# Preparing the first unit of the state space layers between the groups of the gated expert stage before it, and down products one group later in both gated stages

## The reference

```python
x = x + 0.5 * _L1_ffn_ref(_layernorm(x), ...)     # m1a, gated experts
x = x + _L1_attn_ref(_layernorm(x), ...)          # mam, four state space layers
x = x + 0.5 * _L1_ffn_ref(_layernorm(x), ...)     # m1b, gated experts
```

```python
hidden = silu(gate_all) * up_all
out = einsum('nk,nkd->nd', combine, einsum('nke,ked->nkd', hidden, down_proj)) + shared(flat)
```

```python
x_in, z = split(layernorm(x) @ in_w.T)
xc = silu(conv4(x_in) + cb)
dtr, Bm, Cm = split(xc @ xp_w.T)
dt = softplus(dtr @ dt_w.T + dt_b)
h = h * exp(dt * A) + (dt * xc) * Bm     # a scan over the 256 rows, 16 states, 256 channels
y = sum(h * Cm) + xc * D
x = (y * silu(z)) @ out_w.T + x
```

## Time and profile before

| | us |
|---|---|
| median of 3 executions | 2748.93 (2746.9 to 2752.26) |
| profiled execution | 2750.35 |
| its span | 2748.6 |
| TensorE busy | 2499.3 (91%) |
| VectorE busy | 1939.4 (71%) |
| ScalarE busy | 1620.2 (59%) |
| GpSimd busy | 1144.2 (42%) |
| first gated stage, from the first gate product to the last add | 379.97 to 506.03 |
| last add to the second scan | 506.03 to 556.72 |
| state space stage to the second gated one | to 1403.48 |
| second gated stage, from its logits to the last transposes | 1403.48 to 1533.11 |

### The profile page before, as it was taken

The page is one execution under the profiler, slowest core; times in us unless marked ns, Lnnn a source line. Parts: engine busy times, 40 slices in busy tenths (PEclk is TensorE's granted clock), DMA queues, the critical chain, the costliest instruction groups (busy, mean ns, idle before and its releaser), DMA issues. The chain is left out here.

```text
span 2748.6 us, 37972 instructions
## 1 busy us (share of the span) xinstructions
PE 2499.3 (91%) x11190; PEld 1421.5 (52%) x11190; DVE 1939.4 (71%) x3923; ACT 1620.2 (59%) x3505; POOL 1144.2 (42%) x919
## 2 busy tenths in 40 slices
PE   7999978689999999999988899978879998799977
PEld 5766743345555555555434344446644445556655
DVE  6888856399999999999955444356644444587754
ACT  3565522388888888888832344357753443466634
POOL 1000011189999999999930000042310001355432
PEclk9999989899999999999999999979989998999988
DMA  2000023234444444444433112000002110000000
GB/s 105 1 1 1 1 85 74 82 136 157 163 161 154 170 160 164 155 164 160 169 133 81 47 62 96 28 1 1 0 21 89 62 62 27 1 1 0 1 1 16
DMA packets 34618, 205.63 MB, mean 75 GB/s; under 512 B 4000, under 2 KB 5152, under 8 KB 13216
## 3 DMA queue, kind: packets, MB, share of 16 engines
q1 hardware_dynamic: 34464, 203.83, 20.7%
HBM read 201.19 MB, written 2.62 MB: 74 GB/s over the span
## 5 line engine op out<-in xcount | busy, mean ns | idle before, releaser
L1313 POOL TENSOR_TENSOR mam_state_c<-mam_state,weights_r 128x1024 f32<-128x1024 f32 x256 | 599.9, 2362 | 16.1 <-DVE mam_state L1246 15.0
L1246 DVE TENSOR_TENSOR_SCAN mam_state<-banks,mam_dbu 128x1024 f32<-128x1024 f32 x256 | 577.1, 2275 | 1.6 <-ACT banks L1392 0.6
L1496 PE MATMUL banks<-mam_state_c,identity 128*128 128x512 f32 x1024 | 485.1, 607 | 12.3 <-POOL mam_state_c L1313 11.3
L1392 ACT ACTIVATE banks<-mam_dt,mam_a_neg 128x255 f32<-128x255 f32 x1024 | 425.0, 461 | 66.4 <-DVE mam_state L1246 65.9
L1496 PEld LDWEIGHTS banks<-mam_state_c,identity 128*128 128x128 f32 x1024 | 187.1, 190 | 226.1 <-issue 190.6
L1005 PE MATMUL banks<-route_xnt,weights_r 128*128 128x512 f32 x512 | 247.6, 608 | 8.1 <-PEq L69 8.1
L1229 DVE TENSOR_TENSOR mam_dbu<-banks,weights_r 128x1024 f32<-128x1024 f32 x192 | 227.5, 1198 | 8.3 <-ACT banks L1400 8.3
L558 POOL TENSOR_SCALAR route_ln_rs<-route_ln_mv 128x4 f32<-128x4 f32 x16 | 5.1, 316 | 494.6 <-DVE route_ln_mv L636 494.6
L438 ACT ACTIVATE at_probs<-banks,at_nmax 128x256 f32<-128x256 f32 x256 | 117.7, 471 | 138.0 <-DVE at_nmax L379 138.0
L2512 POOL TENSOR_TENSOR at_attention<-at_relu 128x512 f32<-128x512 f32 x128 | 131.0, 1040 | 128.0 <-ACT at_relu L2557 86.5
L959 DVE TENSOR_TENSOR m2b_hidden<-m2b_gelu,m2b_comb_spread 128x512 f32<-128x512 f32 x120 | 80.7, 690 | 116.4 <-ACT m2b_gelu L985 113.7
(11 more groups left out here) (434 smaller groups left out, 5031.9 us busy)
## 6 DMA issues: line engine op xcount, KB each, us to landing
weights_r<-mam_bc_rows SPq DMA_DIRECT2D x128, 1024.0 KB, 4.7
m2a_comb_spread<-m2a_comb_rows SPq DMA_DIRECT2D x15, 1024.0 KB, 8.2
m2b_comb_spread<-m2b_comb_rows SPq DMA_DIRECT2D x15, 1024.0 KB, 7.1
m1a_comb_spread<-m1a_comb_rows SPq DMA_DIRECT2D x14, 512.0 KB, 7.2
m1b_comb_spread<-m1b_comb_rows SPq DMA_DIRECT2D x14, 512.0 KB, 7.2
weights_r<-in_mb SPq DMA_DIRECT2D x1, 4332.0 KB, 13.0
weights_r<-in_m SPq DMA_DIRECT2D x1, 4200.0 KB, 12.8
weights_r<-in_a SPq DMA_DIRECT2D x1, 2632.0 KB, 12.1
```

The costliest lines, as they stand in the source:

```text
L1246: dve.tensor_tensor_scan(flat2(h[:, i % 4, :, :, :]), decay(i), flat2(dbu[:, i % 4, :, :, :]), 0.0, ALU.mult, ALU.add).then_inc(h_ready, 1)
L1313: pool.tensor_tensor(hc[:, j % 4, :, :, :], h[:, j % 4, :, :, :], c_rows(j), ALU.mult).then_inc(hc_ready, 1)
L1392: i = act.activation(decay(j)[:, o + 1:o + S], dt[:, q, c, 1:S], ACT.Exp, scale=aneg[:, l, k:k + 1])
L1496: k = pe.matmul(y_bank(q)[:, :], K.ident[:, :], flat(hc[:, j % 4, n, :, :]), start=(j == 0 and n == 0), stop=(j == NP - 1 and n == 1))
```

## The change

1. In both gated stages the down product of group g-1 stands where that of g stood; copy, transposes and add of a pair move one group later too (e=1, 2, 3).
2. The buffers and semaphores of the state space stage belong to an object made before m1a (`StateSpace`), and its preparation steps are functions (`state_vector`, `state_tensor`, ...), with the same instructions as before.
3. m1a calls these steps between its groups: input statistics and rows by pairs of sequences, unit 0's layernorm, conv, B/C rows and DMA, step sizes, dt and dt_u, unit 1's layernorm rows. GpSimd makes the taps of layer 0 first. The last of the steps stand behind the last pair's groups (p=4).
4. mam keeps the statistics and rows of the last pair, unit 1's transposes, gate product of unit 0, unit 1's taps and conv. Its ScalarE does the first decays before conv and gate instead of after. `before_units` is gone on all engines, and VectorE's `begin` too.

```diff
@@ stage_gated_experts, TensorE
+                def down(g):
+                    p, e = divmod(g, NG)
+                    if e == 0 and p >= 2:
+                        pe.wait_ge(added, p - 1)
+                    pe.wait_ge(hid_ready, g + 1)
+                    pe.matmul(K.ps[4 + p % 2][:, :], DOWN[e], hid[:, g % 3, :], start=(e == 0),
+                              stop=(e == NG - 1)).then_inc(down_done, 1)
                 for p in range(NP + 1):
                     for e in range(NG):
                         g = p * NG + e
                         if p < NP:
                             if 1 < g + 1 < NP * NG:
                                 gate_up(g + 1)
-                            if e == 0 and p >= 2:
-                                pe.wait_ge(added, p - 1)
-                            pe.wait_ge(hid_ready, g + 1)
-                            pe.matmul(K.ps[4 + p % 2][:, :], DOWN[e], hid[:, g % 3, :], start=(e == 0),
-                                      stop=(e == NG - 1)).then_inc(down_done, 1)
-                            if g == 1:
+                        if 0 < g <= NP * NG:
+                            down(g - 1)
+                            if g == 2:
                                 own_spread(3)
-                        if p and e == 1:
+                        if p and e == 2:
                             pe.wait_ge(yt_ready, p)
...
+                        if M:
+                            state_early_tensor(K, M, pe, p, e, R)
@@ stage_gated_experts, GpSimd
                     route_gpsimd(K, R, pool, p)
-                    if tag == "m1a":
-                        conv_taps(K, pool, p)
-                if tag == "m1a":
-                    conv_taps(K, pool, 0)
+                    if M:
+                        conv_taps(K, M, pool, p - 1)
+                if M:
+                    state_early_gpsimd(K, M, pool)
@@ new functions
+def state_early_vector(K, M, dve, p, e, added):
+    if (p, e) == (1, 4):
+        dve.memset(M.xpad[:, :, :], 0.0)
+        dve.memset(M.rows[:, :], 1.0)
+    if (p, e) in ((2, 2), (3, 1), (3, 4)):
+        n = ((2, 2), (3, 1), (3, 4)).index((p, e))
+        dve.wait_ge(added, n + 1)
+        state_input_stats(K, M, dve, n)
+    if (p, e) in ((2, 4), (3, 2), (3, 5)):
+        state_input_rows(K, M, dve, ((2, 4), (3, 2), (3, 5)).index((p, e)))
+    if (p, e) == (2, 6):
+        state_vector(K, M, dve, 2, None, (0, 0, 0))
+    if (p, e) == (3, 3):
+        state_vector(K, M, dve, 2, (0, 0, 0), (0, 1, 1))
+    if (p, e) == (3, 7):
...
+                dve.tensor_scalar(M.skip[:, l, c, :], K.ident[:, :], state_field(K, l, "dsk")[:, c:c + 1], None, ALU.mult)
+    if (p, e) == (4, 4):
+        dve.wait_ge(M.a_exp, M.L + 1)
+        dve.tensor_scalar(M.aneg[:, :, :], M.aneg[:, :, :], -1.0, None, ALU.mult).then_inc(M.constants, 1)
+        state_vector(K, M, dve, 4, (0, 0, 0), None)
+def state_early_gpsimd(K, M, pool):
+    state_input_root(K, M, pool, 0)
+    state_gpsimd(K, M, pool, 3, None, (0, 0, 0))
+    conv_taps(K, M, pool, 3)
+    state_input_root(K, M, pool, 1)
+    state_gpsimd(K, M, pool, 3, (0, 0, 0), (0, 1, 1))
+    state_input_root(K, M, pool, 2)
+    state_gpsimd(K, M, pool, 5, (0, 0, 0), None)
+def state_early_scalar(K, M, act, p, e):
+    if (p, e) == (2, 8):
+        act.wait_ge(K.loaded["mb"], 16)
+        state_scalar(K, M, act, 4, None, (0, 0, 0))
+    if (p, e) == (3, 1):
+        state_scalar(K, M, act, 5, None, (0, 0, 0))
+    if (p, e) == (3, 3):
+        state_scalar(K, M, act, 7, None, (0, 0, 0), False)
+    if (p, e) == (3, 4):
+        state_scalar(K, M, act, 0, (0, 0, 0), None)
+    if (p, e) == (3, 6):
+        state_scalar(K, M, act, 4, (0, 0, 0), (0, 1, 1))
+    if (p, e) == (3, 8):
+        act.preload_act_table_set(EXP_AND_LN)
+        state_scalar(K, M, act, 1, (0, 0, 0), None)
+        state_scalar(K, M, act, 2, (0, 0, 0), None)
+    if (p, e) == (4, 2):
+        state_scalar(K, M, act, 3, (0, 0, 0), None)
...
+def state_early_tensor(K, M, pe, p, e, R):
+    if (p, e) == (3, 1):
...
+        state_tensor(K, M, pe, 5, None, (0, 0, 0))
+    if (p, e) == (3, 2):
+        pe.wait_ge(M.taps_made, 1)
+        state_tensor(K, M, pe, 6, None, (0, 0, 0))
+    if (p, e) == (3, 4):
+        state_tensor(K, M, pe, 0, (0, 0, 0), None)
+    if (p, e) == (3, 5):
+        state_tensor(K, M, pe, 1, (0, 0, 0), None)
+    if (p, e) == (4, 3):
+        state_step_sizes(K, M, pe, 4, (0, 0, 0))
@@ stage_state_space, ScalarE
...
                 act.wait_ge(cleared, 1)
-                before_units(prepare)
-                act.wait_ge(constants, 1)
-                act.wait_ge(dt_ready, 1)
+                state_scalar(K, M, act, 5, None, (0, 1, 1))
                 input_scale(0, 0)
                 decays(0, 0, 0, 0)
+                state_scalar(K, M, act, 7, (0, 0, 0), (0, 1, 1))
                 over_units(act, slot, 5)
```

533 lines of the change are left out of this document (269 added, 264 removed).

## The result

The changed kernel takes 2683.05 us (2682.61 to 2686.15, 4 executions) where the kernel before takes 2749.64 beside it: a ratio of 0.9754, 95% interval 0.9742 to 0.9765, or 66.6 us less. The prediction was 2691, range 2680 to 2709. The profiled execution has a span of 2681.2 us, 67.4 less than the earlier trace rows.

The account below looks back on a forecast made before the run. TensorE bounds the gated stages, idling in waits for hidden tiles; a serial chain fills the 50.7 us between them. 15.5 - 10.8 + 35.7 + 17.0 = 57.4 us saved gives 2691, range 2680 to 2709.

Parts of the forecast that it names:

- D: Second gated stage, down products one group later: 15.7 to 20.2 us less 1.0, taken as 17.0 saved.
- A: First gated stage, down products one group later: TensorE's waits go, gain 13.4 to 17.3 us, 15.5 taken.
- the gate product of t=0: Last pair's second group in the first gated stage: its gate product comes some 15 to 18 us before 480.40.
- B: Early steps in the first gated stage's last pair and tail: the end comes 10.8 us later (5.1 + 5.75).
- C: Between the gated stages: second scan 15.0 us after the stage's end in place of 50.7, 35.7 saved, at half clock.
- the prediction's other branch: Between the stages at full clock: taps take 3.67 us, VectorE's chain ends last, 38.4 us saved.
- The 1.0 that I took off: Second gated stage, last pair: down products catch up with hidden tiles that combine rows delay, 1.0 us less gain.
- The start of the state space layers' later units: Later units of the state space layers: no added time allowed; their taking longer would be a sign of error.
- Rival 1: Gated stages: later down product only moves the wait, to the up product or routing-weight DMA; 2700 to 2724, chance 0.17.
- Rival 2: Last pair: early steps hold the engine queues, two or three waits of 4 us; 2699 to 2709, chance 0.12.
- Rival 3: Last pair: five early TensorE steps each hold the queue over 11.5 us, so slower; 2762 at 14 each, chance 0.02.
- The rule that speaks against the change: VectorE rows beside GpSimd slow from 1.11 to 2.80 us; 0 in the sum, 5.1 higher if biting at three places.

Follow-up runs that it names:

- The filled kernel: Changed kernel plus unread TensorE products at the first gated stage's end, two ahead of the last transposes and three behind the step-size sums: 2689.55 us, ratio 0.9782.
- the second execution of after: The changed kernel, unchanged, timed again against the kernel before: 2684.33 us, ratio 0.9772.
- alone: The kernel before with only the later down products, in both gated stages: 2715.54 us, ratio 0.9879.
- my own version of it: Changed kernel with step sizes moved to VectorE, two steps' decays before the taps, last pair's input rows behind the second scan: 2690.77 us, ratio 0.9778.

## Why the prediction was right

The range held the time, and the sum of the steps, 57.4, stands against 60.3 in the core stretch. The mechanisms of the four parts came as described, but for a detail of D. The whole saving, 66.6 us, is 9.2 more than forecast: 2.9 are the sizes of the parts. The rest, 7.1 by the two profiled executions, lies in stretches that the change leaves alone, and that is luck. Point by point:

- **A, 15.5; measured 17.3.** The mechanism was right and the size was the upper end that the working had, 17.3: the restarts behind short waits went too. The forecast of 15 to 18 us at the gate product of t=0 reads 18.86 in the trace, but 0.91 of that is an earlier start of the stage and 0.86 a down product that now stands behind it.
- **B, -10.8; measured -12.2.** From the own rows to the last down product's start 5.6 us more than without the early steps (forecast 5.1); from there to dt_u's end 9.78 for the 3.19 of before, 6.6 more (forecast 5.75). The mis-sized term is the clock: I had taken transposes and sums at full speed, and they stood behind 1.73 us of idle time and ran at a mean clock of 0.57 up to the third sum. The filled kernel has 1.6 less from transposes to dt_u's end, and so has the kernel with the early preparation alone.
- **C, 35.7; measured 37.4.** The order of what ends last was right (ScalarE's decays, 15.0 forecast, 13.26 measured). The taps took 4.92, not 5.9, since the half clock lasted only for a part, and transposes and gate product 1.5, not 2.4. The filled kernel has 12.24 at full clock, the 12.3 that the prediction's other branch implies, and VectorE's input term ends last there, as that branch had it.
- **D, 17.0; measured 17.9**, 18.2 in the second execution of after, 15.1 alone; the difference is the wait for the first pair's combine rows and the half clock behind it. The 1.0 that I took off stood in the wrong place: I had it in the last pair, whose only wait is one of 0.27 that before has too, and after's wait of 0.76 is in the first.
- **What it did not have**: 7.1 us in stretches that the change does not touch. 4.4 of them are TensorE's clock at the gelu stage's start, which took 15.91 us in another execution of the same program; the cause of the other 2.7 is open, and two executions of one program differ in these places by 2.4 and 1.3 us. The start of the state space layers' later units, of which I had allowed nothing, took 0.14 more.

Rival 1 is real in one pair of the second stage, 0.5 to 2.0 us and up to 1.7 more by the clock. Rival 2 shows in the early steps without the later down products, 1.7 us. Rival 3 did not come: TensorE waits for no early step in the last pair. The rule that speaks against the change did not bite in it (the sets of rows that were read took 1.11 to 1.12, where GpSimd was idle), but it did in my own version of it. The row there is 4.48 us for four VectorE rows beside GpSimd. The Trainium skill (SBUF — State Buffer, "Who interferes with whom") says that where VectorE is in a two-port mode, whichever of the two engines issues first has the shared ports for its whole instruction and the other blocks. The trace agrees: the first row starts under GpSimd's product that ends at 510.88 and ends at 510.97; the second starts at 510.89, behind the start of the next product, and ends at 513.28, that product at 513.19; the other two then take 0.33 each.

## What to carry to other kernels

A product that waits for a chain on other engines can get one more group of independent work in front of it: the gain here was the idle time and the restarts, and the cover that it gives can be measured by delaying the chain. A serial preparation can go into the stage before, where it cost 12.2 us here and saved 37.4; its last links (sums on TensorE and a copy that waits behind a table load) stand on the path, and moving them to an engine that is free there, with one more step's decays ahead of the taps, gave 4.6 to 5.0 more up to the last scan. Small steps of VectorE cost nothing beside its own work here, but four times as much beside GpSimd's. And a gain of a few us is to be looked for in a stretch of the trace and not in the median: the stages' starts alone moved that by more.
